# Attention pooling over 32 chunks of rows: weighted sums three chunks behind the scores, the odd tile shared by four quadrants, candidates loaded as columns

## The reference

```python
W_b, W_c = (fc1_w[:E], fc1_w[E:])
h = relu(einsum('bse,eh->bsh', behavior_emb, W_b) + (candidate_emb @ W_c)[:, None, :] + fc1_b)
scores = einsum('bsh,h->bs', h, fc2_w[:, 0]) + fc2_b[0]
attn = softmax(scores, axis=-1)
user_interest = einsum('bse,bs->be', behavior_emb, attn)
x = concatenate([user_interest, candidate_emb], axis=1)
z = relu(x @ mlp1_w + mlp1_b)
logit = (z @ mlp2_w + mlp2_b)[:, 0]
```

## Time and profile before

| what | us |
|---|---|
| median of 3 runs (lowest, highest) | 270.85 (269.1, 280.69) |
| the profiled execution | 268.94 |
| its span, first to last instruction | 267.2 |
| outside of the span | 1.74 |
| granted clock of PE over the span | 1.000 |

### The profile page before, as it was taken

One profiled execution on the slowest core, in us unless ns is written; L12 is line 12 of the kernel. 1 busy time (PEld: TensorE's weight loads), 2 busy tenths in 40 slices (PEclk: granted clock), 3 DMA queues, 4 the chain that ended last, 5 costly groups with the idle time before them and its releaser, 6 DMA issues.

```text
span 267.2 us, 10126 instructions
## 1 busy us (share of the span) xinstructions
PE 262.0 (98%) x3762; PEld 215.1 (81%) x3762; DVE 219.3 (82%) x400; ACT 204.4 (76%) x484; POOL 43.3 (16%) x38
## 2 busy tenths in 40 slices
PE   8999999999999999999999999999999999999995
PEld 7558778888888888888888888888888888888873
DVE  0468988888899988888898888899988888998641
ACT  3567788888889887888888788888888888888402
POOL 2002212110121212012121210112121112212100
PEclk9999999999999999999999999999999999999999
DMA  7999999999999999999999999999999999999600
GB/s 242 425 426 424 420 423 424 426 426 427 427 418 425 427 427 425 429 425 429 429 429 427 422 420 427 427 429 425 425 429 429 427 427 427 420 424 427 274 5 2
DMA packets 10940, 105.87 MB, mean 396 GB/s; under 512 B 1200, under 2 KB 2096, under 8 KB 2992
## 3 DMA queue, kind: packets, MB, share of 16 engines
q1 hardware_dynamic: 10640, 105.51, 93.9%
q10 hardware_dynamic: 288, 0.20, 0.2%
HBM read 105.70 MB, written 0.00 MB: 396 GB/s over the span
## 4 chain that ended last, share of the span: by engine, by line
PE 88%; DMA 9%; issue 1%; DVE 1%; ACT 0%; DVEq 0%; POOL 0%; ACTq 0%; POOLq 0%
PE z_ps L613 18%; PE s_ps L632 16%; PE u_ps L642 16%; PE z_ps L614 15%; PE z_ps L617 15%; DMA xt<-in_behavior_t 9%; PE z_ps L608 2%; PE z_ps L750 1%; PE z_ps L642 1%; PE u_ps L674 1%; PE z_ps L714 1%; PE z_ps L720 1%; DVE hidden L464 0%; ACT xh L329 0%; PE z_ps L700 0%
## 5 line engine op out<-in xcount | busy, mean ns | idle before, releaser
L329 ACT CAST xh<-xt 128x800 fp32r<-128x800 f32 x120 | 101.2, 867 | 26.6 <-DMA xt<-in_behavior_t 24.5
L454 DVE TENSOR_TENSOR xl<-xt,xh 128x800 fp32r<-128x800 f32 x120 | 116.1, 987 | 1.9 <-ACT xh L329 1.6
L371 ACT ACTIVATE hidden<-z_ps,bias 128x200 f32<-128x200 f32 x256 | 88.6, 429 | 16.2 <-PE z_ps L617 13.7
L613 PE MATMUL z_ps<-xh,w_hi 128*128 128x512 f32 x240 | 87.5, 365 | 1.0 <-DVE hidden L464 1.0
L614 PE MATMUL z_ps<-xh,w_lo 128*128 128x512 f32 x240 | 79.5, 346 | 0.0
L296 POOL TENSOR_TENSOR weights_by_row<-weights,masks_sb 128x400 f32<-128x400 f32 x31 | 41.5, 1337 | 208.0 <-ACT weights L336 208.0
L464 DVE TENSOR_TENSOR hidden<-z_ps,neg_bias 128x800 f32<-128x800 f32 x64 | 63.2, 987 | 3.0 <-PE z_ps L608 1.7
L617 PE MATMUL z_ps<-xl,w_hi 128*128 128x512 f32 x240 | 63.1, 344 | 0.0
L613 PEld LDWEIGHTS z_ps<-xh,w_hi 128*128 128x128 f32 x240 | 45.1, 188 | 16.2 <-issue 7.5
L642 PE MATMUL u_ps<-x,weights_by_row 128*32 128x128 f32 x1500 | 50.7, 273 | 0.0
L632 PE MATMUL s_ps<-hidden,f_col 128*3 128x160 f32 (+4 forms) x1280 | 50.3, 301 | 0.0
(11 more groups left out here) (68 smaller groups left out, 81.4 us busy)
## 6 DMA issues: line engine op xcount, KB each, us to landing
x<-in_behavior SPq DMA_DIRECT2D x32, 1600.0 KB, 26.0
xt<-in_behavior_t SPq DMA_DIRECT2D x30, 1600.0 KB, 24.0
xt<-in_behavior_t SPq DMA_DIRECT2D x4, 400.0 KB, 4.9
xt<-in_behavior_t SPq DMA_DIRECT2D x2, 800.0 KB, 8.0
later_sb<-in_later SPq DMA_DIRECT2D x1, 258.5 KB, 22.7
cand<-in_candidate SPq DMA_DIRECT2D x1, 192.0 KB, 5.9
first_sb<-in_first ACTq DMA_DIRECT2D x1, 128.0 KB, 3.9
masks_sb<-in_masks SPq DMA_DIRECT2D x1, 114.0 KB, 4.5
```

Of the source, the lines that this page charges most:

```text
L329: nc.scalar.copy(xh[g][:, :], xt[q][:, g, :]).then_inc(xh_made, 1)
L371: op = nc.scalar.activation(hidden[q % 2][:, g, :, mine], z[:, :, mine], ACT.Relu, bias=bias[:, bass.ds(c * ROWS + g * EACH + b, 1)])
L454: nc.vector.tensor_tensor(xl[g][:, :], xt[q][:, g, :], xh[g][:, :].bitcast(F32), ALU.subtract).then_inc(xl_made, 1)
L613: nc.tensor.matmul(z[:, a:b], w_hi[:, :], xh[g][:, a:b], start=True, stop=False)
```

## The change

The sums run three chunks behind (`LAG = 3`) and not two; SP's pairs become `xt` of c and `x` of c - 3, and at the start `xt` of 2 and 3 are issued ahead of `x` of 0. The sum of chunk 29 leaves the loop for the end. The loop's hardware part still covers the same code, with periods 0 to 6 written out (`FIRST` = 7). Tile 24 of each sum is done as four matmuls of 32 columns, one on each quadrant, behind tile 3 (behind tile 13 in the last chunk). `transpose_sums` moves from behind g = 3 of its period to between g = 1 and the scores of the next period, and writes beside the hidden products in the bank of g = 1 (`beside_z`, columns 800 to 831); ACT's copy of it moves ahead of the relu of g = 1. The candidates come from the host as columns (`cand_t`, the first 128 with `w_c`, the others in one load), so the turning and the copying go. `shifts` is one step in period 1. At the end the products of the MLP's candidate part for the first 28 chunks stand behind the sum of chunk 31.

```diff
-FIRST_COLS = {"ident": P, "w_c": P}
+FIRST_COLS = {"w_c": P, "cand_t": 4 * P}
-        FIRST = 3
+        FIRST = 7
+        def beside_z(q, g):
+            return z_view(q, g)[:, WIDTH:WIDTH + 2 * ROWS]
...
@@ SP
-                if g == 0:
-                    sp.dma_start(cand[:, 0:1, :], candidate_v[:, 0:1, :]).then_inc(cand_loaded[0], 16)
-                if g == 1:
-                    sp.dma_start(masks_sb[:, :], masks).then_inc(masks_loaded, 16)
-            sp.dma_start(cand[:, 1:, :], candidate_v[:, 1:, :]).then_inc(cand_loaded[1], 16)
+            sp.dma_start(cand_t[:, P:], cand_rest).then_inc(cand_rest_loaded, 16)
...
+                if half == 0:
+                    sp.dma_start(masks_sb[:, :], masks).then_inc(masks_loaded, 16)
             for c in range(2, X_BUFS):
                 load_transposed(c, None)
-                load(c - 2, None)
+            load(0, None)
...
-                    load(c - 2, (j + 2) % X_BUFS)
-            load(LAST - 1, X_BUFS - 2)
-            load(LAST, X_BUFS - 1)
+                    load(c - LAG, (j - LAG) % X_BUFS)
+            for c in range(CHUNKS - LAG, CHUNKS):
+                load(c, c % X_BUFS)
@@ ACT
                 act.wait_ge(z_done, c * GROUPS + (g + 1))
+                if g == 1 and phase > LAG + 1 and (q - LAG) % 2 == 0:
+                    copy_pooled_t(c - LAG - 1, beside_z(q, g))
...
-            copy_candidates(0)
...
                 if phase == 0:
-                    bias_times_f2(0)
                     positive_bias(0)
                     biased_relu(c, q, 1, phase)
-                    copy_candidates(1)
                     biased_relu(c, q, 3, phase)
+                    bias_times_f2()
+                    positive_bias(1)
                     return
-                flush = phase >= 2 and (q - 2) % 2 == 1
+                flush = phase > LAG and (q - LAG) % 2 == 1
                 biased_relu(c, q, 1, phase)
+                if phase == 1:
+                    exponents(0, 0, True)
                 next_half(0)
                 next_half(1)
+                if flush:
+                    copy_pooled4(c - LAG, u_ps)
                 if phase == 1:
-                    bias_times_f2(1)
-                    positive_bias(1)
-                if flush:
-                    copy_pooled4(c - 2, u_ps)
-                exponents(c - 1, (q + 1) % 2, phase <= 2)
-                next_half(2)
-                biased_relu(c, q, 3, phase)
-                if flush:
-                    copy_pooled_t(c - 2, u_ps)
+                    biased_relu(c, q, 3, phase)
+                    next_half(2)
+                else:
+                    exponents(c - 1, (q + 1) % 2, phase <= 2)
+                    next_half(2)
+                    biased_relu(c, q, 3, phase)
                 next_half(3)
@@ PE
+                def tile(g, t, cols):
+                    return nc.tensor.matmul(
+                        bank[g * Q:(g + 1) * Q, cols], weights_by_row[buf][:, t, :],
+                        x[q][:, t * E + cols.start:t * E + cols.stop], start=buf == 0 and t < GROUPS,
+                        stop=buf == 1 and WHOLE_TILES - GROUPS <= t < WHOLE_TILES, tile_position=(0, g * Q))
                 for t in range(a, b):
...
+                    op = tile(t % GROUPS, t, slice(0, E))
+                    if t == odd_after:
+                        for last in range(WHOLE_TILES, TILES):
+                            for g in range(GROUPS):
+                                tile(g, last, slice(g * Q, (g + 1) * Q))
...
                     if phase == 0 and g == 0:
-                        pe.wait_ge(first_loaded, 16)
-                        transpose_candidates(0)
-                    if phase == 0 and g == 1:
                         bias_products(0)
-                    if phase == 0 and g == 2:
-                        shift_sums(0)
                     if phase == 0 and g == 3:
-                        transpose_candidates(1)
-                    if phase == 1 and g == 1:
                         bias_products(1)
+                    if phase == 1 and g == PHASE_AT:
+                        shift_sums()
...
+                    if g == PHASE_AT and phase > LAG + 1 and (q - LAG) % 2 == 0:
+                        transpose_sums(c - LAG - 1, beside_z(q, g))
                     if g == PHASE_AT and phase >= 1:
                         score(c - 1, (q + 1) % 2, phase == 1)
-                    if g == PHASE_AT and phase >= 2:
-                        weighted_sum(c - 2, (q + 2) % X_BUFS, phase == 2)
-                    if g == GROUPS - 1 and phase >= 2 and (q - 2) % 2 == 1:
-                        transpose_sums(c - 2, u_ps)
+                    if g == PHASE_AT and phase >= LAG:
+                        weighted_sum(c - LAG, (q - LAG) % X_BUFS, phase == LAG)
 
             periods(period)(pe)
+            pe.wait_ge(later_loaded, 16)
             row_sums(0)
+            weighted_sum(LAST - 2, (LAST - 2) % X_BUFS, False)
+            score(LAST, LAST % 2, False)
+            transpose_sums(LAST - 2, u_ps[:, P:P + 2 * ROWS])
+            spread_inverses(0)
             weighted_sum_alone(LAST - 1)
-            score(LAST, LAST % 2, False)
-            mlp_candidates(0, 0)
-            spread_inverses(0)
-            mlp_candidates(0, 1)
             mlp_candidates(1, 0)
-            mlp_candidates(1, 1)
             row_sums(1)
             weighted_sum_alone(LAST)
             spread_inverses(1)
-            transpose_sums(LAST, last_pair_ps)
+            mlp_candidates(0, 0)
+            mlp_candidates(0, 1)
+            mlp_candidates(1, 1)
+            transpose_sums(LAST, last_pair_ps[:, P:P + 2 * ROWS])
             mlp_pooled(0, 0)
```

More of the change, by code:

```diff
@@ L27 @@
 RUNS = TILES // RUN
+WHOLE_TILES = TILES - TILES % GROUPS
 X_BUFS = 4
@@ L34 @@
 WHOLE = 2
+LAG = 3
 WARM_UP = 9
@@ L56, with attention_pooling_kernel @@
 Z_SLOTS, Z_BACK = rotation(Z_BUFS, Z_SHORT)
-def attention_pooling_kernel(nc, behavior, behavior_t, candidate, weights_1, first, masks, later, out):
+def attention_pooling_kernel(nc, behavior, behavior_t, cand_rest, weights_1, first, masks, later, out):
     B, S, E = behavior.shape
@@ L156, in attention_pooling_kernel @@
         masks_loaded = sem("masks_loaded")
-        cand_loaded = [sem(f"cand_loaded{i}") for i in range(2)]
+        cand_rest_loaded = sem("cand_rest_loaded")
         later_loaded = sem("later_loaded")
@@ L268, in _ @@
                 load_transposed(c, c - X_BUFS)
-                load(c - 2, None if c - 2 < X_BUFS else c - 2 - X_BUFS)
+                load(c - LAG, None if c - LAG < X_BUFS else c - LAG - X_BUFS)
             with sp.Fori(0, CHUNKS // X_BUFS - 2) as turn:
@@ L309, in _ @@
             act.dma_start(weights_1_sb[:, :], weights_1).then_inc(weights_1_loaded, 16)
-            act.dma_start(first_sb[:, :], first).then_inc(first_loaded, 16)
+            act.dma_start(first_sb[:, 0:2 * P], first).then_inc(first_loaded, 16)
             act.wait_ge(setup_step, 1)
@@ L342, in copy_pooled4, with copy_pooled_t, bias_times_f2 @@
                 nc.scalar.copy(pooled4[:, :], bank[:, 0:P]).then_inc(pooled4_copied, 2)
-            def copy_pooled_t(c, bank):
+            def copy_pooled_t(c, summed):
                 act.wait_ge(pooled_t_done, c + 1)
[L346 to L351, removed]
+                nc.scalar.copy(pooled_t[:, bass.ds((c - 1) * ROWS, 2 * ROWS)], summed).then_inc(pooled_t_copied, 2)
+            def bias_times_f2():
+                act.wait_ge(setup_step, 3)
                 act.wait_ge(neg_f2_made, 1)
-                nc.scalar.mul(bias_f2[:, a:b], neg_bias[:, a:b], neg_f2[:, :]).then_inc(bias_f2_made, 1)
+                nc.scalar.mul(bias_f2[:, :], neg_bias[:, :], neg_f2[:, :]).then_inc(bias_f2_made, 1)
             def positive_bias(part):
@@ L435, in negative_bias, with shifts @@
                                         ALU.add, ALU.mult).then_inc(setup_step, 1)
[L437 to L444, removed]
+            def shifts():
+                dve.wait_ge(shift_done, 1)
+                dve.wait_ge(masks_loaded, 16)
+                nc.vector.tensor_tensor(shift_sel[:, :, :],
+                                        u_ps[:, 0:P].rearrange("p (c r) -> p c r", r=EACH),
+                                        own_row.unsqueeze(1).to_broadcast([P, CHUNKS, EACH]),
                                         ALU.mult).then_inc(shift_step, 1)
-                dve.wait_ge(shift_step, 3 * part + 1)
-                nc.vector.reduce_sum(shift[:, a:b], shift_sel[:, a:b, :], axis=AX.X).then_inc(shift_step, 1)
-                dve.wait_ge(shift_step, 3 * part + 2)
-                nc.vector.tensor_scalar(shift[:, a:b], shift[:, a:b], b2, None, ALU.add).then_inc(shift_step, 1)
+                dve.wait_ge(shift_step, 1)
+                nc.vector.reduce_sum(shift[:, :], shift_sel[:, :, :], axis=AX.X).then_inc(shift_step, 1)
+                dve.wait_ge(shift_step, 2)
```

(30 more changed lines are left out.)

57 lines of the change are left out of this document (19 added, 38 removed).

## The result

The changed kernel takes 283.81 us (median of 6; 281.52 to 284.54), the kernel before 269.48 (median of 6). The ratio is 1.051, with an interval of 1.046 to 1.056: slower by 5%. I had forecast 266.6. One of the six executions of the kernel before took 280.69, and the ratio leaves it out. The profiled execution takes 283.63, its span is 281.8. The granted clock is not the cause: the two executions of the changed kernel at 1.000 took 281.5 and 281.9, the four at 0.994 took 283.6 to 284.5.

A forecast was written before the change was run, and what follows sets the result against it. PE was taken to bound the kernel by a hair, the loads right behind and DVE's ring close. Span 267.2 - 3.7 (loop) + 1.4 (end) = 264.9, plus 1.74 outside: 266.6 us, range 262.8 to 269.6.

The forecast's parts named there:

- Order of the loads: SP's load queue: each `xt` has one load of `x` less ahead of it and lands 3.84 us earlier.
- The loop: Periods 4 to 31: PE 7.58, DVE's ring 7.60, loads 7.683; scores of period 31 at 243.4, 3.7 us ahead.
- DVE's ring: DVE's chain from scores to the max of g = 2 and on to the next scores: 7.50 us.
- Start: First periods: nothing gained at period 3, scores at 30.7; period 4 at 38.2, 1.1 us ahead of before.
- Odd tile: Each sum on PE: sharing the odd tile over four quadrants gains 0.12 us, bounds 0 to 0.16.
- B: Rival, chance 0.16: the odd tile gains nothing, periods stay 7.60 and 7.79, time 269.4 us.
- C: Rival, chance 0.04: the four narrow matmuls run one after the other, PE's period becomes 8.36, time 290.7 us.
- Turning in front: Turning of the sums ahead of the scores: adds 0.2 us to DVE's ring in every second period, bounds 0 to 0.24.
- Loads' bound: End of the loop: `xt` of chunk 31 lands at 237.6, so its scores start no earlier than 242.7.
- End: From the scores of period 31 on: -0.4 + 0.5 - 0.12 + 1.46 = +1.4 us.
- Rival A: Rival, chance 0.25: the end costs nothing and the loads alone bound the loop, time 264.2 us.
- Sum: Whole kernel: 267.2 - 3.7 + 1.4 = 264.9 us of span, with 1.74 outside 266.6 us.

The follow-up runs named there:

- late-mask run: The changed kernel with POOL's mask of chunk c also waiting for DVE's low half 1 of chunk c + 2 (chunk 30 excepted): 267.06 us, ratio 0.990.
- run with the turning behind: The changed kernel with POOL's mask waiting for low half 1 and the turning back behind g = 3: 267.17 us, ratio 0.991.

## Why the prediction was wrong

The step that failed is one that I did not write down. Under "Order of the loads" I moved the landings 3.84 us forward and asked what the *late* side would do. I did not ask what the wait of ACT for those landings had been holding back. Under "The loop" DVE's ring of 7.50 us was taken as fixed, with 1.89 for low halves 0 and 1. It is 1.89 only while the mask starts behind low half 0; else it is 2.57, and the ring 7.50 + 0.68 = 8.18, where 8.165 was measured. POOL had no term anywhere in the sum. The clue was in the trace of before: the mask took 1337 ns in the mean on the page and 872 at the least in the view of its line, so it was waiting inside its own record.

The Trainium skill (SBUF — State Buffer, "Who interferes with whom") says that a DVE instruction with two SBUF inputs contends with a POOL instruction that reads SBUF, that the pair of ports they share is an exclusive lock, and that the order of issue decides which of the two blocks. The rows agree: 0.98 becomes 1.66 behind a mask of 0.87, and the max, with one input from PSUM, takes 0.98 beside a mask. I had not weighed it.

With the mask out of the way, the late-mask run tests the other steps one by one; its scores start at 30.89 in period 3, 38.84 in period 4, 151.91, and 244.07 in period 31.

- *Start*: 30.7 and 38.2 predicted, 30.89 and 38.84 measured; the granted clock was 0.76 from 28 to 35, and the scores of period 3 took 2.09 us and not 1.57. In the changed kernel itself the pair at 26.23 was already 2.56, PE stood still for 1.84 us ahead of 29.75, and the scores of period 3 began at 32.05 and took 2.02.
- *Odd tile*: right. Scores to the next hidden product is 2.87 (138.14 to 141.01) against 3.00: 0.13, 0.12 taken. Rivals B and C are out; the measured time lies between theirs (269.4 and 290.7), and by the mechanism of neither. The 56 passes start between 139.52 and 140.81, 23 ns apart in the mean. The Trainium skill's 25 ns (TensorE: Matmul & The Clock Gate, "Wait — 56ns, not 53.3ns?") is not a floor for them.
- *Turning in front*: 0.2 in every second period was too much. From 38.84 to 151.91, 15 periods are 7.54 each, where I had 7.60, and the run with the turning behind is no faster.
- *Loads' bound*: right in kind. ACT waits for landings again from 115.93 on, and from 151.91 on 12 periods are 7.68 each. `xt` of chunk 31 lands at 238.90, 2.7 us ahead of before, where one load less and the identity were to give 4.0. The scores follow 5.17 later (5.1 taken).
- *End*: span 265.3 - 244.07 = 21.2 against 20.14: +1.1, where I had +1.4. The last turn comes at 259.12, behind the two products as said. Rival A, an end that costs nothing, is out. (I had read the scores of chunk 31 before as starting at 254.31. That row has 37 of the 40 passes, and the first three start at 254.15; no sum changes by it.)
- *Sum*: 244.07 against 243.4, 267.04 for the profiled execution against 266.6. The sum was that of a kernel in which POOL costs nothing. That it comes within 0.5 us is in part luck: periods of 7.54 and not 7.60, landings 1.3 us later than forecast and an end 0.3 us cheaper cancel.

For the changed kernel: 28 periods of 8.165 instead of 7.60 are 15.8 us, the start 1.35 more, and the scores of period 31 start at 260.66, 17.3 after the forecast. That is, within 0.1 us, the difference of 17.2 between 283.8 and 266.6.

Of the change's gain, 1% is left with a late mask (0.990, interval 0.987 to 0.993). Whether it needs the third chunk is not fully shown: the two runs with two chunks, odd tile and late mask were not faster than before (271.6 and 270.4), but stalls at their start stand in the way. The best kernel here is the changed one with the mask behind low half 1, at 267.06. It beats the kernel before and the changed one; the runs with the exponents later (267.26) and with the turning behind (267.17) can't be told from it.

## What to carry to other kernels

Before making data come earlier, list what the wait for it holds back: an engine that is released early issues its followers early, and one of these can take something that a third engine needs at that moment. An instruction of one shape on an idle engine whose mean time is well above its minimum may be waiting inside its record, as the mask was (1337 against 872 ns); see for what, and who would wait if the order turned round. Where two engines exclude each other, fix the order with a semaphore instead of leaving it to who happens to be late.

## What the hardware showed that was not expected

- The exclusion goes by order: low half 1 took 0.98 us alone or ahead of a mask and 1.66 behind one; the mask 0.87 alone and 1.40 behind a low half. The first of the two kept its time to within 0.1 us, and only the second was held.
- One binary can have executions at two times: 270.1 and 284.9 (odd tile alone), 270.9 and 284.3 (loads as before), 271 and 283 (two chunks behind). In the slow profiles of the first two the periods are 8.1 to 8.2 us to the end, in the fast profile of the third 7.68. None of the three was profiled at both times.
- PE stood still for 1.7 to 2.8 us at a time in early passes of the short hardware loop, with no releaser in the profile, in the two profiles with the odd tile shared and three periods written out. With seven written out, in the run of the same kernel, it was under 1 us at a time. The cause stays open.
